# Latent attention with dispatch: another order of the steps on four engines

## The chip, the cores and the metric

The kernel runs on one core of one Trainium2 chip, as one program. The metric is the device time of a run in microseconds (us). TensorE (PE) does matrix products, VectorE (DVE) and ScalarE (ACT) do elementwise work and reductions and can read PSUM, GpSimd (POOL) works on SBUF and issues the indirect DMAs, SyncE (SP) issues plain DMAs. Each engine runs its own instructions strictly in their written order and waits on semaphores for the others.

## The reference

Activations x are 32 batches of 128 rows by 128 channels; a context is 32 x 128 x 96. Six residual stages follow each other, each on the layernorm of x. The fifth and the sixth are the ones the change concerns:

```
x = x + attn0(ln(x)); x = x + xattn0(ln(x), ctx); x = x + experts0(ln(x)); x = x + causal_attn(ln(x))
x = x + latent(ctx, ln(x), mask)      # 2 heads of 64; keys: 128 context rows + 128 rows of x itself
        q, k, v from layernorms; q and k RMS-normalised; softmax over 256 keys; times Wo
x = x + relu_moe(ln(x))               # router: 8 experts, top 2; relu(x w1 + b1) w2 + b2, gated sum
```

## The kernel before

The setup, four earlier stages and then the function `latent_attention` run one after the other. `latent_attention` works batch by batch (n from 0 to 31) and some steps by groups G of four batches. Beside the attention it does the dispatch for the last stage: it normalises the finished rows, computes router logits, ranks each row within its expert and scatters the rows to a DRAM buffer `routed`, where tiles of 256 rows of one expert are then read back by the last stage (`relu_experts`: 39 tiles, two products with four slices each, and two indirect DMAs per tile that write the results to `returned`).

The order on each engine is written out in a table, `ORDERS["latent"]`. An entry such as `K+2` in round n does step K of batch n+2, in each round. An entry such as `C^10` does the step of a group once, in the round where n+10 is the first batch of the group; for the steps `L`, `R`, `R1`, `EX`, `GG` and `PL` it is done for a unit of the router, in the round where n minus the number is the unit's last batch. The router's units are groups 0 and 1, 2 and 3, 4 and 5, 6, and 7. The loop goes over n from -14 to 55, on all engines with the same table, but each engine has its own n: nothing but semaphores ties the rounds together. A later round on POOL can therefore run at the same time as an earlier round on PE.

Per batch the steps on PE are P (L1707 to L1709, projections of x and of the context), K (L1767, three transposes of unit keys and queries), s (L1775 and L1777, scores and mask for the maximum), m (L1795, transpose of the maxima), T (L1707 to L1709 with q and k, the transposed scores), f (L1800, subtracts the maximum), w (L1811, probabilities by values), o (L1818, transpose of the heads), y (L1823 and L1824, output product). Per group: C and X (L1719, transposes of the normalised inputs), Z (L1726, transposes of the rows to be routed). Per unit: L (L1735, router logits, one product with a 128x8 output per batch, which the trace records as two) and R (L1743 and L1746, ranks by a triangular matrix). The semaphores that bind PE: T waits for `q_lo` and `k_lo`, K for `unit` of its batch and `k_lo` of the batch before, w for the exponentials.

The steps of the others that are spoken of: DVE R1 (L2090 to L2120, the router's choice of two, 14 instructions), sp (L2038, spreads the maximum), d (L2018, `q_heads`), M (L2026), n (L2047, L2049, heads), a (L2032), u (L2009, `unit`), ss (L1996 and L2001, `norms` and `norms_kept`), kl (L2056, `k_lo`), zm and zs (moments and shift of the finished rows), PL (places; for unit 2 also the list of the first 16 tiles), GG (gates, and labels into the rows). ACT kh (L1881 and L1882, rounded keys and queries), e (L1873 and L1874), zn (L1926, writes the normalised rows into a ring of four buffers), rp, zk (L1938). POOL rs (L2287 to L2295), iv (L2316, `inverse`), ql (L2309, `q_lo`), lc and lx (L2302, `c_lo` and `x_lo`), zr (L2326 and L2329), sc (L2339, two indirect DMAs of one batch).

The dispatch is bound by these waits: sc of batch n waits for PL and GG of its unit and for rp of its group. zn of group G waits, from group 4 on, until all scatters of group G-4 have landed, since it takes their buffer. SP starts the first 16 tiles when the scatters of groups 0 to 5 have landed (`EARLY_GROUPS = 6`). On POOL the sends of the last stage stand behind all 64 scatters.

Of the kernel before, what the change touches and what calls it, by code (L numbers as in the profile page):

```python
# [17 lines left out]
ACT, ALU, AX = mybir.ActivationFunctionType, mybir.AluOpType, mybir.AxisListType  # L18

P = 128  # L20
# [91 lines left out]
def load_setup(nc, x, weights, cols, rows, consts, later, sb, sem, ready, routed):  # L112

    with ExitStack() as ctx:
# [102 lines left out]
    },  # L217
    "latent": {
# [4 lines left out]
    },  # L223
}

# [2333 lines left out]
```

## Time and profile before

| | us |
|---|---|
| median of 3 runs | 1393.14 |
| lowest and highest | 1386.01, 1399.97 |
| profiled execution, its own time | 1390.87 |
| its span, first to last instruction | 1389.1 |
| attention and dispatch, first instruction to the last scatter of group 5 | 952 to 1203 |
| busy over the span: PE, DVE, ACT, POOL | 1192.9, 883.4, 677.0, 776.2 |

Of the span, 952 us belong to the stages in front, which the change does not touch, then some 250 us to attention and dispatch up to the first tile, and the rest to the tiles and the final sums. The share of busy time is therefore read stage by stage. A row of the timeline gives start and length in us, the engine, the source line, what is written and read, and in brackets how long the engine sat idle before and for whom. A row of the windows gives the busy time of each engine in one stretch and the clock granted to TensorE as a share of its full speed. Matmuls overlap, so the time of a step on PE is the distance between starts.

### The profile page before, as it was taken

The page shows a single profiled execution, that of the slowest core. Times are in us where ns is not written, and L with a number is a line of the kernel's source. Part 1 is how long each engine was busy: PE and PEld are TensorE (multiplying, and loading weights), DVE is VectorE, ACT ScalarE, POOL GpSimd, SP SyncE. Part 2 cuts the span into 40 slices and gives each one's busy share as a digit, 9 for nine tenths or more (in the row PEclk, how much of TensorE's full clock was granted, in tenths as well). Part 3 has the DMA queues.
Part 4 walks back from the last instruction along what each step waited for, and adds up shares of the span by engine and source line. Part 5 has one row for each costly group of instructions (what it writes and reads, how often), then busy time and mean ns, then how long its engine had stood idle before and what let it go on. Part 6 is the DMA issues. An engine that isn't in the chain of part 4 may idle for free. (4 is left out here: it accounts for less than half of the span.)

```text
span 1389.1 us, 34193 instructions
## 1 busy us (share of the span) xinstructions
PE 1192.9 (86%) x12731; PEld 902.3 (65%) x12731; DVE 883.4 (64%) x2024; ACT 677.0 (49%) x1304; POOL 776.2 (56%) x878
## 2 busy tenths in 40 slices
PE   1899998888888876999789999994799998399992
PEld 0577776656555555666457777773699997388882
DVE  3688876579999985677335665663688876422223
ACT  1344544434455433455334555544778653155561
POOL 3787775555555633444355655642676676765552
PEclk9999999689999997999958999997899897599996
DMA  9920000000000000000000000000000000366665
GB/s 345 381 79 2 3 2 8 9 15 15 21 16 15 10 9 1 1 1 1 1 1 2 3 2 3 2 3 15 17 13 7 11 23 32 124 202 202 196 196 187
DMA packets 51571, 75.46 MB, mean 54 GB/s; under 512 B 13118, under 2 KB 31683, under 8 KB 51152
## 3 DMA queue, kind: packets, MB, share of 16 engines
q1 hardware_dynamic: 43344, 60.57, 13.8%
q0 software_dynamic: 4544, 8.47, 1.8%
q10 hardware_dynamic: 3520, 4.23, 0.9%
q8 instruction: 104, 1.70, 0.5%
q14 instruction: 59, 0.48, 0.1%
HBM read 40.37 MB, written 31.70 MB: 52 GB/s over the span
## 5 line engine op out<-in xcount | busy, mean ns | idle before, releaser
L597 DVE TENSOR_REDUCE maxes<-bank 128x8 f32<-128x1024 f32 x192 | 234.4, 1221 | 58.7 <-PE bank L396 57.4
L524 ACT ACTIVATE self_probs<-bank 128x1024 f32<-128x1024 f32 x128 | 129.1, 1022 | 45.6 <-PE bank L428 45.2
L1468 POOL DMA_INDIRECT returned<-relu_y,relu_slots x78 | 76.3, 979 | 68.8 <-DVE relu_y L1444 54.8
L1405 ACT ACTIVATE relu_hidden<-bank,cols 128x256 f32<-128x256 f32 x156 | 73.8, 473 | 77.6 <-PE bank L1364 77.6
L738 POOL TENSOR_TENSOR self_k_hi_m<-self_kq_hi,const 128x512 fp32r<-128x512 f32 x64 | 66.5, 1039 | 80.0 <-ACT self_kq_hi L552 80.0
L531 ACT ACTIVATE self_neg_max<-bank 128x512 fp32r<-128x512 f32 x64 | 38.2, 596 | 148.0 <-PE bank L442 148.0
L1364 PE MATMUL bank<-latent_kq,relu_w_tile 128*128 128x256 f32 x312 | 94.8, 387 | 0.5 <-DVE latent_kq L1438 0.5
L1372 PE MATMUL bank<-relu_hidden,relu_w_tile 128*128 128x256 f32 x312 | 93.1, 381 | 0.0
L607 DVE RECIPROCAL self_recip<-bank 128x128 f32<-128x128 f32 x64 | 61.2, 956 | 31.6 <-PE bank L455 29.3
L1438 DVE COPY latent_kq<-bank 128x256 f32<-128x256 f32 x39 | 16.6, 425 | 100.5 <-PE bank L1354 98.1
L603 DVE TENSOR_SCALAR bank<-bank 128x1024 f32<-128x1024 f32 x64 | 78.2, 1223 | 3.3 <-PE bank L416 3.3
L738 POOL TENSOR_TENSOR causal_q_lo_m<-causal_kq_lo,const 128x512 fp32r<-128x512 f32 x32 | 33.3, 1040 | 80.5 <-PE bank L428 80.4
L2339 POOL DMA_INDIRECT routed<-latent_rows,latent_place_i x64 | 63.7, 995 | 24.4 <-issue 22.6
L455 PE MATMUL bank<-self_probs,values 128*32 128x128 f32 x2048 | 73.6, 287 | 1.4 <-ACT self_neg_max L531 1.2
L455 PE MATMUL bank<-self_probs,head_ones 128*32 128x128 f32 x2048 | 71.3, 282 | 0.0
L428 PE MATMUL bank<-self_neg_max,const_r 32*128 32x512 f32 x256 | 62.3, 478 | 9.2 <-DVE bank L603 5.7
L455 PEld LDWEIGHTS bank<-self_probs,values 128*32 128x32 f32 x2048 | 55.3, 114 | 18.9 <-issue 16.2
L524 ACT ACTIVATE causal_probs<-bank 128x1024 f32<-128x1024 f32 x64 | 64.5, 1021 | 6.0 <-PE bank L428 3.4
L738 POOL TENSOR_TENSOR self_q_lo_m<-self_kq_lo,const 128x512 fp32r<-128x512 f32 x64 | 66.5, 1039 | 0.4 <-PE bank L428 0.2
L738 POOL TENSOR_TENSOR self_q_hi_m<-self_kq_hi,const 128x512 fp32r<-128x512 f32 x64 | 66.4, 1038 | 0.0
L442 PE MATMUL bank<-ident,maxes 128*128 128x128 f32 x384 | 65.5, 295 | 0.6 <-POOL maxes L761 0.3
L1372 PEld LDWEIGHTS bank<-relu_hidden,relu_w_tile 128*128 128x128 f32 x312 | 59.7, 192 | 8.4 <-ACT relu_hidden L1405 0.2
(395 smaller groups left out, 3501.8 us busy)
## 6 DMA issues: line engine op xcount, KB each, us to landing
relu_w_tile<-in_w_ffn SPq DMA_DIRECT2D x39, 512.0 KB, 3.5
routed<-blank SPq DMA_DIRECT2D x1, 19760.0 KB, 61.2
relu_slots<-routed SPq DMA_DIRECT2D x39, 130.0 KB, 3.1
x_all<-in_x SPq DMA_DIRECT2D x8, 256.0 KB, 8.4
x_before<-x_all SPq DMA_DIRECT2D x8, 256.0 KB, 2.3
relu_back<-returned SPq DMA_DIRECT2D x4, 512.0 KB, 8.0
latent_mask_rows<-returned ACTq DMA_DIRECT2D x4, 512.0 KB, 8.7
self_ctx_in<-in_ctx SPq DMA_DIRECT2D x8, 192.0 KB, 2.5
```

Source lines behind the costliest of these rows:

```text
L428: mm = pe.matmul(t_bank(u), cr[rows_of(u), C_ONES + u * P:C_ONES + (u + 1) * P], neg_max[n % 2][rows_of(u), :], start=False, stop=True, sk ...
L442: mm = pe.transpose(OM[:, j * P:(j + 1) * P], maxes[n % 2][:, j * P:(j + 1) * P], sb["ident"][:, :])
L455: mm = pe.matmul(OM[rows_of(u), c:c + P], of(u, j), probs[n % 2][:, u, j, :], start=j == 0, stop=j == U - 1)
L524: act.activation(probs[n % 2][:, 2 * pair:2 * pair + 2, :, :].rearrange("p u j q -> p (u j q)"), T[:, 2 * pair * GT:(2 * pair + 2) * GT], ...
L597: dve.tensor_reduce(out.rearrange("p j u -> p u j"), S.rearrange("p (u j k) -> p u j k", u=2, j=U), AX.X, ALU.max, negate=True).then_inc(m ...
L603: dve.tensor_scalar(t, t, CLAMP / scale, -CLAMP / scale, ALU.min, ALU.max).then_inc(clipped, 1)
L738: pool.tensor_tensor(out[n % 2][:, :, :], src[(n // GB) % 2][:, batch_cols(n)].bitcast(F32).unsqueeze(1).broadcast_to([P, U, P]), slots.un ...
L1364: pe.matmul(HT[i % 2][:, 0:TT], w_tile[t % NW][:, c * P:(c + 1) * P], s[t % 2][:, :], start=True, stop=True)\
L1372: pe.matmul(YT[t % 2][:, 0:TT], w_tile[t % NW][:, F1 + c * P:F1 + (c + 1) * P], hidden[i % C1][:, :], start=c == 0, stop=c == C1 - 1).then ...
L1405: act.activation(hidden[i % C1][:, :], HT[i % 2][:, 0:TT], ACT.Relu, bias=sb["cols"][:, bass.ds(r + (COL_RELU + c), 1)]).then_inc(hidden_d ...
L1468: pool.indirect_dma_start(returned[:, :], bass.IndirectOffsetOnAxis(ap=slots[t % NX][:, b, P:P + 1].bitcast(I32), axis=0), y[t % NY][:, b, ...
L2339: pool.indirect_dma_start(routed[:, :], bass.IndirectOffsetOnAxis(ap=place_i[u % 3][:, k, b:b + 1], axis=0), rows[G % 4][:, k, n % GB, :], ...
```

## The change

Only the table `ORDERS["latent"]` changes. No instruction is added, removed or resized. On every engine the steps of a round stand in another order, and some are moved by one or more rounds. On POOL the scatter's number goes from 20 to 23.

```diff
     "latent": {
-        "PE": "T+0 m+0 K+2 w-1 y-2 f+0 L^-9 Z^-11 R^-10 P+5 C^10 o-1 s+2 X^9",
-        "ACT": "cp+4 ln^10 hc^8 ax^8 zn^-11 cn^11 sq+4 hx^8 kh+2 e+0 rp^-17 zk^-11 v+5 oc-1 EX^-10 ac^10",
-        "DVE": "mx^13 zs^-8 sp+0 d+2 M+1 n-1 a-2 u+3 ss+4 kl+2 zm^-5 PL^-10 R1^-9 GG^-11 mc^13",
-        "POOL": "lc^6 lx^5 ql+0 iv+2 rs^11 sc-20 zr^-7",
+        "PE": "K+2 m+0 w-1 T+0 C^9 y-2 L^-9 f+0 P+5 o-1 s+2 X^9 R^-10 Z^-10",
+        "ACT": "cp+4 zn^-9 hc^8 ax^8 kh+2 sq+4 ac^9 e+0 oc-1 hx^8 rp^-17 cn^11 EX^-10 ln^10 zk^-10 v+5",
+        "DVE": "R1^-10 sp+0 d+2 M+1 zs^-8 PL^-11 n-1 a-2 u+3 kl+2 ss+4 mc^13 GG^-11 mx^14 zm^-5",
+        "POOL": "lc^4 iv+0 rs^9 sc-23 ql-1 zr^-10 lx^4",
     },
```

The first place is PE around the ranks of unit 0 (R). In the kernel before, from the end of one T to the next P:

```order
L1709 MATMUL bank<-latent_q_hi,latent_k_lo 128x256
L1795 MATMUL bank<-ident,latent_maxes 32x128
L1767 MATMUL bank<-ident,latent_unit 128x128 x3
L1811 MATMUL bank<-latent_v,latent_probs 128x65 x4
L1823 MATMUL bank<-rows,latent_one 128x128
L1824 MATMUL bank<-raw_xattn,latent_o_t 128x128
L1800 MATMUL bank<-latent_neg_max,const_r 128x256 x2
L1743 MATMUL bank<-latent_both,const_r 128x64
L1746 MATMUL bank<-latent_both,const_r 128x56
```

In the changed kernel, from the end of s and the start of R:

```order
L1775 MATMUL bank<-latent_k_hi,latent_q_hi 128x256
L1777 MATMUL bank<-latent_mask_rows,const_r 128x128
L1743 MATMUL bank<-latent_both,const_r 128x64
L1746 MATMUL bank<-latent_both,const_r 128x56
```

R stood behind m, K, w, y and f; now it stands behind s, with K, m and w after it and then T. T itself has moved from the head of the round to between w and y, in every round, so that K, m and w stand between s and T, and only y, L and f between T and P.

The second place is POOL at group 2, behind the reciprocal deviations (rs) of group 3; the piece of the difference:

```order
 L2295 TENSOR_TENSOR latent_shift_ln<-latent_shift_ln,latent_rstd 128x8
+L2309 TENSOR_TENSOR latent_q_lo<-latent_q_heads,latent_q_hi 128x256
 L2302 TENSOR_TENSOR latent_c_lo<-latent_cf,latent_c_hi 96x512
-L2309 TENSOR_TENSOR latent_q_lo<-latent_q_heads,latent_q_hi 128x256
-L2316 TENSOR_TENSOR latent_inverse<-latent_norms_kept,latent_power 128x6
+L2316 TENSOR_TENSOR latent_inverse<-latent_norms_kept,latent_power 128x6
+L2309 TENSOR_TENSOR latent_q_lo<-latent_q_heads,latent_q_hi 128x256
 L2302 TENSOR_TENSOR latent_x_lo<-latent_xf,latent_x_hi 128x512
```

`q_lo` is now ahead of `c_lo` and of `x_lo`. The third place is POOL around the scatter of the batch that closes group 1 (the second row of each, two DMAs) and zr of group 5. Before:

```order
L2316 TENSOR_TENSOR latent_inverse<-latent_norms_kept,latent_power 128x6
L2339 DMA routed<-latent_rows,latent_place_i 38912x130 x2
L2326 TENSOR_SCALAR latent_z_var_eps<-latent_z_mean_var 128x4
L2329 TENSOR_TENSOR latent_z_rstd<-latent_z_var_eps,latent_power 128x4
L2309 TENSOR_TENSOR latent_q_lo<-latent_q_heads,latent_q_hi 128x256
```

Now:

```order
L2316 TENSOR_TENSOR latent_inverse<-latent_norms_kept,latent_power 128x6
L2339 DMA routed<-latent_rows,latent_place_i 38912x130 x2
L2309 TENSOR_TENSOR latent_q_lo<-latent_q_heads,latent_q_hi 128x256
L2326 TENSOR_SCALAR latent_z_var_eps<-latent_z_mean_var 128x4
L2329 TENSOR_TENSOR latent_z_rstd<-latent_z_var_eps,latent_power 128x4
```

zr has moved behind `q_lo`. The `inverse` in the first row is that of batch 29 before and of batch 30 now: since iv, ql and sc all changed their numbers, by 2, 1 and 3, the scatters and zr are one batch later against the work of the attention, not three.

## Rows read from the trace of the kernel before

**Rows 1.** Windows: engines' busy times, granted clock (PEclk), DMA share, GB/s.

```profile
core 0: us, PE busy (x) PEld busy (x) DVE busy (x) ACT busy (x) POOL busy (x), PEclk, DMA share, GB/s
1020.00:1040.00 20.00, 19.90 (x147) 18.02 (x146) 17.96 (x66) 16.24 (x51) 13.98 (x18) 1.00 0.02 5
...
1078.00:1080.00 2.00, 2.00 (x10) 2.00 (x10) 1.61 (x6) 0.00 (x0) 1.83 (x2) 0.50 0.03 8
...
1088.00:1090.00 2.00, 2.00 (x10) 2.00 (x9) 1.90 (x13) 0.42 (x4) 1.57 (x3) 0.50 0.00 0
...
1180.00:1200.00 20.00, 7.02 (x30) 6.31 (x30) 12.65 (x77) 3.59 (x9) 13.28 (x14) 0.50 0.45 149
```

**Rows 2.** Timeline of PE, two w steps in a row, plain rounds.

```profile
1032.86 1.00 PE L1811 MATMUL bank<-latent_v,latent_probs 128*128 128x65 f32 x8
...
1037.76 1.00 PE L1811 MATMUL bank<-latent_v,latent_probs 128*128 128x65 f32 x8
```

**Rows 3.** Timeline of PE, w steps with L and R between them.

```profile
1074.61 1.00 PE L1811 MATMUL bank<-latent_v,latent_probs 128*128 128x65 f32 x8
...
1084.34 1.12 PE L1811 MATMUL bank<-latent_v,latent_probs 128*128 128x65 f32 x8
...
1086.79 1.15 PE L1746 MATMUL bank<-latent_both,const_r 128*128 128x56 f32 x9
...
1092.03 1.00 PE L1811 MATMUL bank<-latent_v,latent_probs 128*128 128x65 f32 x8
...
1126.29 1.95 PE L1735 MATMUL bank<-cols,latent_x_t 128*128 128x8 f32 x16
1132.32 1.03 PE L1811 MATMUL bank<-latent_v,latent_probs 128*128 128x65 f32 x8
...
1139.91 1.00 PE L1811 MATMUL bank<-latent_v,latent_probs 128*128 128x65 f32 x8
```

**Rows 4.** Timeline at the start of the attention: POOL, DVE, PE.

```profile
993.68 1.26 POOL L2302 TENSOR_TENSOR latent_c_lo<-latent_cf,latent_c_hi 96x512 fp32r<-96x512 f32 x1
994.91 0.73 POOL L2309 TENSOR_TENSOR latent_q_lo<-latent_q_heads,latent_q_hi 128x256 fp32r<-128x256 f32 x1
995.61 1.32 POOL L2316 TENSOR_TENSOR latent_inverse<-latent_norms_kept,latent_power 128x6 f32<-128x6 f32 x1
...
995.75 0.42 DVE L2018 TENSOR_TENSOR latent_q_heads<-bank,latent_head_gamma 128x256 f32<-128x256 f32 x1 [1.84 <-POOL latent_q_lo L2309]
...
997.09 1.50 DVE L2009 TENSOR_TENSOR latent_unit<-latent_kq,latent_inverse 128x384 f32<-128x384 f32 x1
...
997.23 0.33 PE L1818 MATMUL bank<-ident,latent_heads 128*128 128x128 f32 x1 [1.10 <-DVE latent_heads L2049]
...
999.72 0.52 PE L1767 MATMUL bank<-ident,latent_unit 128*128 128x128 f32 x3 [0.88 <-DVE latent_k_lo L2056]
```

**Rows 5.** Timeline where scatters, `x_lo` and the norms meet: DVE, POOL, PE.

```profile
1111.18 1.72 DVE L2001 TENSOR_SCALAR latent_norms_kept<-latent_norms 128x6 f32<-128x6 f32 x1
...
1111.53 1.29 POOL L2302 TENSOR_TENSOR latent_x_lo<-latent_xf,latent_x_hi 128x512 fp32r<-128x512 f32 x1
...
1113.37 0.52 PE L1767 MATMUL bank<-ident,latent_unit 128*128 128x128 f32 x3 [0.59 <-DVE latent_k_lo L2056]
```

**Rows 6.** Timeline of the end of the attention: PE, then POOL.

```profile
1164.08 0.66 PE L1726 MATMUL bank<-ident,latent_rows 128*128 128x128 f32 x4
...
1208.12 0.66 PE L1354 MATMUL bank<-ident,relu_slots 128*128 128x128 f32 x2 [12.65 <-DMA relu_slots<-routed]
...
1175.90 0.19 POOL L2326 TENSOR_SCALAR latent_z_var_eps<-latent_z_mean_var 128x4 f32<-128x4 f32 x1 [5.36 <-DVE latent_z_mean_var L2070]
...
1182.75 1.06 POOL L2339 DMA_INDIRECT routed<-latent_rows,latent_place_i  x1 [5.54 <-issue]
...
1201.95 0.96 POOL L2339 DMA_INDIRECT routed<-latent_rows,latent_place_i  x1 [0.30 <-issue]
```

**Rows 7.** DMA issues: count, median us from issue to landing.

```profile
routed<-latent_rows,latent_place_i POOLq DMA_INDIRECT x64, 2.4
```

## The prediction, as it was put on record before the result

> **What bounds the kernel now.** I read the windows first, to see which stage has idle engines. In plain rounds of the attention TensorE is busy 19.90 of 20 us at full clock, VectorE 17.96, POOL 13.98 [rows 1]. A round there takes 4.90 us, the distance of two w steps [rows 2]. The order of work cannot shorten that: no matmul is removed, and TensorE waits for nothing. What is left to win or lose is where TensorE idles or runs slowly, and there are four such places.
>
> The first is the start, where the chain of waits goes over POOL, VectorE and TensorE: q_lo at 994.91 stands behind c_lo, VectorE sits idle 1.84 us for it, and TensorE is idle 1.10 us before o and 0.88 us before K [rows 4]. The second is the granted clock. It falls to 0.50, the lower level of 1.2 GHz, in the rounds that hold L and R, although TensorE is busy 2.00 of 2.00 us there [rows 1]. The third is one round in the stretch of the scatters, where TensorE is idle 0.59 us before K [rows 5]. The fourth is the end, from the last attention step to the first tile at 1208.12, where TensorE had been idle 12.65 us for the first rows read back [rows 6], at half clock and busy 7.02 of 20 us [rows 1].
>
> **The change, part by part.** The sum is made against the profiled execution, 1390.87 us with a span of 1389.1, which is 2.3 us under the median of 1393.14.
>
> *Ranks and the clock.* In the order before, the steps m, K, w, y, f and then L or R follow each other between the dense products T and P. All these are small outputs, one-row weights or transposes. The w steps around R are 1084.34 and 1092.03, 7.69 us apart, and again 1132.32 and 1139.91, 7.59 apart [rows 3]. A plain round is 4.90 [rows 2] and R takes 1.15 of it [rows 3], so 6.05 would be the price at full clock and 1.64 and 1.54 us are lost to the half clock, 3.2 in all. Now R stands behind s, and K, m and w follow, then T. The run of small work around R shrinks from m, K, w, y, f, R to R, K, m, w. Two of its six parts are gone and dense work stands on both sides. I take it that these two falls go: **minus 3.2 us**. The bounds are 0, if they stay, and a gain of 3.2.
>
> *Logits and the clock.* L stood behind m, K, w, y, f, now behind y alone, in front of f. The w steps around the first L are 1074.61 and 1084.34 [rows 3], 9.73 us apart; 4.90 for the round [rows 2] and 1.95 for an L at full clock [rows 3] make 6.85, so 2.9 us are lost to the fall. L itself is the longest stretch of tiny outputs in the kernel and its neighbours on both sides are still y and f. I take 0, since the L step is untouched in length, and keep a gain of 5.8 (two units) as a bound.
>
> *The start.* q_lo of batch 2 passes ahead of c_lo and comes 994.91 - 993.68 = 1.23 us earlier; q_heads, the maximum and the heads behind it on VectorE follow. But T and m used to run before K, and now K is the first step of the round. K waits for the unit keys, whose inverse still stands behind c_lo: 995.61 + 1.32 = 996.93, then 1.50 for the product [rows 4] and about 0.4 for k_lo, now directly behind it, about 998.8. Before, K began at 999.72. TensorE is 0.9 us earlier at K, but still has T to do, some 0.7 us. I take **minus 0.5**, with 0 and 2.0 (the two idle times) as bounds. On VectorE k_lo now stands in front of the two norms, which costs the inverse of a later batch 0.4 us; the inverse is wanted a round later.
>
> *The collision at 1111.* norms_kept takes 1.72 us while x_lo runs on POOL for 1.29, and k_lo and K queue behind it [rows 5]. Now k_lo is in front of the norms, so such a collision no longer reaches K, and x_lo is behind q_lo. **Minus 0.6**, bounds 0 and 0.8.
>
> *K at the head of each round.* K is asked for about 0.8 us (T and m) earlier in its round, and k_lo comes earlier by the norms that it passed. Where the unit product meets a POOL instruction it takes up to 1.50 us [rows 4] instead of some 0.55, and then K may wait a few tenths. **Plus 0.5**, bounds 0 and 3 (a tenth in each of 30 rounds).
>
> *The scatters.* Against the attention's own steps they move by one batch, not by three. When the attention ends POOL thus has one more batch to send, two DMAs of 1.28 us each by the 15 distances between the 16 issues from 1182.75 to 1201.95 [rows 6]: 2.6 us. POOL sits idle 5.36 and then 5.54 us before the scatter of batch 16 at 1182.75 [rows 6], because places and gates of unit 2 are late, not POOL. 2.6 of 10.9 us are hidden. The 16 scatters from there to 1201.95 decide when the tiles start and are the same as before, and so is the order of L, R, R1, PL and GG among themselves behind the last batch. Cost 0. If the cover were gone, it would be 2.6. zr is one batch later too; its user, the shift on VectorE, now meets it nearly at once, but stands behind d, which waits for the same q_lo. Cost 0.
>
> *The last rounds.* There a round waits for the exponentials. The rows' transpose Z of group 5, at 1164.08 [rows 6], stood between the last f and w and now falls into the wait of the round before. It takes some 0.5 us, so **minus 0.5**, bounds 0 and 0.5.
>
> *ScalarE.* Normalisations move behind the keys and the exponentials. TensorE did not wait for them in plain rounds, so 0.
>
> The sum is -3.2 - 0.5 - 0.6 + 0.5 - 0.5 = **-4.3 us**: 1386.6 in the profiled execution, 1388.8 against the median. I forecast **1389**.
>
> One rule speaks against the largest term. TensorE showed no idle time in the windows where its clock fell [rows 1]. The Trainium skill, page "TensorE: Matmul & The Clock Gate", section "HAM oscillation — how this bites in real kernels", lays such falls to gaps in which the array waits idle. By that rule moving work that is already gapless wins nothing, and the sum would be 1.1 us instead of 4.3. The trace disagrees with it in so far as the falls came without a gap; what it would take to avoid them no row shows.
>
> **The rivals.**
>
> *The falls stay.* The clock could go by what L and R are, not by what stands before them. For it: both rounds with R and both with L show a fall, and none of the plain ones. Against it: R is a shorter step than L, and its fall is separate from that of L, with full clock in between. The time is then 1393.1 - 1.1 = 1392.
>
> *More falls go.* If the breaking up of the small work is what counts, the two L rounds are helped as well: 5.8 us more, and the logits of unit 2 perhaps 1.5. 1389 - 7.3 = 1381.5. Against it: y, L and f still stand together.
>
> *New falls (slower).* In plain rounds P, o, s and T were one dense run, and T is now cut off from it and stands alone between w and y. No plain round of the kernel before has T there, so nothing shows that the clock holds. A fall costs about 1.6 us by the rounds with R. The gain of 4.3 is used up by three falls. With one in every second round, 14 of them, it is 14 x 1.6 = 22 us less 1: about 1414; with one per group of four, 7 x 1.6 - 1 = +10, 1403. Against it: the same work is done in the same 4.90 us, and its longest run of small steps gets shorter. I take 1403 as this rival's time.
>
> *ScalarE held by the ring (slower, small).* zn of groups 4 and 5 stood in a round where its buffer's scatters had long landed; it is now two rounds earlier, in front of kh and e, and the scatters are a batch later. The landing takes 2.4 us [rows 7], and by my count some 2 us are left at each. Were POOL 5 us later than I reckon, 3 us would be lost twice, and the sum would be +2: 1395.
>
> **How the numbers follow.** Chances: my forecast 0.44 (1389), the falls stay 0.28 (1392), more falls go 0.13 (1381.5), new falls 0.08 (1403), ScalarE held 0.07 (1395). A median of three runs moves too: the runs before reach from 1386 to 1400. Eight in ten are in 1379 to 1399, which takes in the bounds of the sum (all gains without L: -6.5; none and K's full cost: +3), the case of more falls and that of the ring, and leaves out most of the new falls. About one per cent, 14 us, is what can be told from no change. Faster than 1379.2 needs the third case and a lucky median: 0.08. Slower than 1407 needs the new falls in more than every fourth round: 0.05. The rest, 0.87, is the same within 1%.
>
> **What would show it.** In the profile of the changed kernel the first step holds if the window after R shows clock 1.00 and the w steps around R are about 6.1 us apart; it fails if 0.50 stands there. The rounds with L should still show 9 to 10 us. K should show no idle time for k_lo in the stretch of the scatters. The scatter of batch 16 should still follow idle time on POOL, and begin some 4 us earlier than 1182.75; if POOL is busy up to it, the scatters have become the bound. Clock 0.50 in plain rounds is the fourth case, and ScalarE idle before zn for a DMA the fifth. The prediction is wrong as a whole if the plain round is not 4.90 us, since everything rests on the order leaving that alone.

## The result

The changed kernel takes 1411.43 us (median of 3 runs, 1404.64 to 1417.99), against 1393.14 before: ratio 1.0152, 95% interval 1.0095 to 1.0208. A second measurement gave 1.0103 (1.0044 to 1.0163); the execution profiled there took 1426.97 us, over 1.5% above the fastest of its kernel, and is not in that ratio. The change is slower by 1.0 to 1.5%, where I forecast no change.

The profiled execution of the changed kernel is its slowest run, 1417.99 us with a span of 1416.2, which is 27.1 us over the span before. Before, the attention's first w step stood at 993.6 and its last at 1165.0, 171.4 us; now 997.96 and 1192.40, 194.4 us. That is 23.0 of the 27.1. The attention starts 5.4 us later, in stages that the change does not touch, and the remaining pieces add up to -1.3. So the question is what happened between the first w and the last.

### The profile page after: what moved, and what is told of

It reads as the page before. It is cut to its first block and busy times, and to the rows that moved or that the text cites. A ratio compares the mean times of both kernels' runs of the same rounds, so it can differ in the third digit from the quotient of the medians.

```text
span 1416.2 us, 34193 instructions
## 1 busy us (share of the span) xinstructions
PE 1221.5 (86%) x12731; PEld 925.2 (65%) x12731; DVE 883.7 (62%) x2024; ACT 677.2 (48%) x1304; POOL 777.4 (55%) x878
## 5 line engine op out<-in xcount | busy, mean ns | idle before, releaser
L738 POOL TENSOR_TENSOR self_q_lo_m<-self_kq_lo,const 128x512 fp32r<-128x512 f32 x64 | 66.6, 1040 | 3.0 <-PE bank L428 2.8
L442 PEld LDWEIGHTS bank<-ident,maxes 128*128 128x128 f32 x384 | 43.9, 148 | 33.9 <-issue 28.0
```

The lines of the kernel that those rows point to most:

```text
L442: mm = pe.transpose(OM[:, j * P:(j + 1) * P], maxes[n % 2][:, j * P:(j + 1) * P], sb["ident"][:, :])
L738: pool.tensor_tensor(out[n % 2][:, :, :], src[(n // GB) % 2][:, batch_cols(n)].bitcast(F32).unsqueeze(1).broadcast_to([P, U, P]), slots.un ...
```

## The profile after

The page of the changed kernel. Second line: the granted clock in 40 slices of 35.4 us.

```profile
PE 1221.5 (86%) x12731; PEld 925.2 (65%) x12731; DVE 883.7 (62%) x2024; ACT 677.2 (48%) x1304; POOL 777.4 (55%) x878
PEclk9999999689999996999859999996799777599996
```

TensorE is busy 28.6 us longer than before with the same 12731 instructions; VectorE, ScalarE and POOL are within 1.2 us of before. TensorE did not wait more, it worked more slowly. The windows of the attention say where (columns as in [rows 1]):

```profile
1000.00:1020.00 20.00, 18.05 (x79) 15.63 (x78) 11.45 (x35) 11.03 (x34) 8.68 (x8) 0.62 0.04 11
...
1040.00:1060.00 20.00, 19.80 (x143) 17.59 (x143) 18.18 (x62) 17.19 (x56) 14.16 (x17) 1.00 0.05 11
...
1100.00:1120.00 20.00, 20.00 (x90) 18.33 (x90) 10.58 (x42) 10.70 (x33) 5.37 (x6) 0.57 0.00 1
...
1160.00:1180.00 20.00, 19.84 (x103) 17.44 (x104) 12.23 (x42) 7.63 (x24) 10.04 (x12) 0.70 0.04 14
```

Between 1040 and 1060 all is as before. Between 1100 and 1120 TensorE is busy 20.00 of 20 us and does 90 matmuls instead of some 145. Closer, in windows of 3 us:

```profile
1090.00:1093.00 3.00, 3.00 (x25) 2.84 (x24) 2.77 (x6) 0.69 (x2) 2.85 (x4) 1.00 0.04 8
1093.00:1096.00 3.00, 3.00 (x19) 2.94 (x18) 2.59 (x13) 2.56 (x10) 1.32 (x1) 0.57 0.00 0
...
1105.00:1108.00 3.00, 3.00 (x16) 2.94 (x16) 1.90 (x6) 1.50 (x5) 0.39 (x1) 0.50 0.00 0
...
1114.00:1117.00 3.00, 3.00 (x17) 2.94 (x15) 1.19 (x3) 2.81 (x10) 0.00 (x0) 0.50 0.00 0
1117.00:1120.00 3.00, 3.00 (x19) 2.44 (x19) 1.11 (x5) 1.54 (x4) 1.94 (x3) 0.95 0.03 8
```

The clock falls to 0.50 (1.2 GHz) about 1093.4 and comes back at 1117.3: 24 us without a moment of idle time. In the kernel before it fell at L and once more at R, and each time it was back in 3 to 7 us. The timeline of TensorE over this stretch, w steps with what stands between them, after two w steps of plain rounds:

```profile
1045.06 1.00 PE L1811 MATMUL bank<-latent_v,latent_probs 128*128 128x65 f32 x8
1049.97 1.04 PE L1811 MATMUL bank<-latent_v,latent_probs 128*128 128x65 f32 x8
...
1087.55 1.00 PE L1811 MATMUL bank<-latent_v,latent_probs 128*128 128x65 f32 x8
...
1089.99 1.85 PE L1735 MATMUL bank<-cols,latent_x_t 128*128 128x8 f32 x16
...
1094.80 1.81 PE L1811 MATMUL bank<-latent_v,latent_probs 128*128 128x65 f32 x8
...
1102.99 2.06 PE L1746 MATMUL bank<-latent_both,const_r 128*128 128x56 f32 x9
...
1105.82 1.81 PE L1811 MATMUL bank<-latent_v,latent_probs 128*128 128x65 f32 x8
...
1113.84 1.07 PE L1726 MATMUL bank<-ident,latent_rows 128*128 128x128 f32 x4
...
1115.56 1.81 PE L1811 MATMUL bank<-latent_v,latent_probs 128*128 128x65 f32 x8
```

The plain round is 4.91 us, against 4.90 [rows 2]. The distances from 1087.55 on are 7.25 (with L), 11.02 (with R) and 9.74 us (with Z), against 9.73, 7.69 and 5.33 before. The R of 1102.99 takes 2.06 us instead of 1.15 [rows 3]: it is inside the slow stretch. The same comes again at the L of 1144.77, with the distances 7.40, 11.02 and 9.74. The 23.0 us, worked out from the distances of the w steps of both kernels:

| rounds | before | after | more |
|---|---|---|---|
| 2 to 5 of the attention | 23.6 | 31.3 | 7.7 |
| the four from the first L on | 28.4 | 34.7 | 6.2 |
| the four from the second L on | 25.1 | 33.2 | 8.1 |
| the last four | 15.8 | 16.9 | 1.1 |
| the other 15 | 78.5 | 78.4 | -0.1 |

The first line is the start. There K waits for k_lo, and behind it the clock falls for 20 us (the window 1000 to 1020 above). POOL, VectorE and TensorE:

```profile
999.71 1.28 POOL L2302 TENSOR_TENSOR latent_c_lo<-latent_cf,latent_c_hi 96x512 fp32r<-96x512 f32 x1
1000.95 1.32 POOL L2316 TENSOR_TENSOR latent_inverse<-latent_norms_kept,latent_power 128x6 f32<-128x6 f32 x1
...
1002.30 1.14 DVE L2009 TENSOR_TENSOR latent_unit<-latent_kq,latent_inverse 128x384 f32<-128x384 f32 x1 [1.02 <-POOL latent_inverse L2316]
...
1003.92 0.52 PE L1767 MATMUL bank<-ident,latent_unit 128*128 128x128 f32 x3 [1.85 <-DVE latent_k_lo L2056]
```

The idle time itself, 1.85 us, is as long as the 1.10 and 0.88 of before together [rows 4]. Between 1006 and 1190 TensorE waits for almost nothing; the view of waits gives in total, times and longest:

```profile
PE bank L1795 <- ACT latent_o_t L1951: 0.6, 2, 0.3
PE bank L1823 <- DVE latent_neg_max L2038: 0.4, 2, 0.2
```

K's wait of [rows 5] is gone. The end of the attention, TensorE and then POOL:

```profile
1192.40 1.97 PE L1811 MATMUL bank<-latent_v,latent_probs 128*128 128x65 f32 x8 [0.49 <-ACT latent_probs L1874]
...
1236.10 0.66 PE L1354 MATMUL bank<-ident,relu_slots 128*128 128x128 f32 x2 [12.02 <-DMA relu_slots<-routed]
...
1204.51 0.20 POOL L2326 TENSOR_SCALAR latent_z_var_eps<-latent_z_mean_var 128x4 f32<-128x4 f32 x1 [4.38 <-DVE latent_z_mean_var L2070]
...
1211.37 1.06 POOL L2339 DMA_INDIRECT routed<-latent_rows,latent_place_i  x1 [5.54 <-issue]
```

From the last w to the first tile it is 43.7 us, and was 43.1. POOL is idle 4.38 and 5.54 us before the scatter of batch 16, as in [rows 6]: it was not held up by the one batch more that it had to send.

## The experiments

Eighteen runs, in five groups, the kernels of a group on one chip with the kernel before. On the chip of the second group all kernels ran some 24 us longer, the kernel before 1417.43, so only ratios to it are compared. "Mean clock" below is the granted clock over 30 us from L on; (1 - clock) x 2 x 30 is the time at 0.50.

The yardstick, the kernel before and the changed one at the first and the second L:

```profile
1077.00:1107.00 30.00, 30.00 (x191) 28.14 (x191) 23.73 (x78) 20.46 (x65) 18.18 (x18) 0.83 0.03 11
1126.00:1156.00 30.00, 29.79 (x196) 27.09 (x196) 23.58 (x86) 14.70 (x48) 22.36 (x24) 0.89 0.08 26
```

```profile
1090.00:1120.00 30.00, 30.00 (x144) 27.30 (x143) 18.43 (x67) 15.65 (x48) 11.49 (x13) 0.60 0.01 2
1145.00:1175.00 30.00, 29.95 (x141) 27.14 (x140) 18.84 (x70) 12.21 (x40) 17.31 (x18) 0.60 0.06 19
```

Before 0.83 and 0.89: 10 and 7 us at 0.50, in two pieces each. Changed 0.60 and 0.60: 24 us each.

### T alone, each way

Between T and P of the changed kernel C stands too, once in four rounds, beside y, L and f, and X, R and Z stand between s and K in some rounds. All of them stay there in e1, the changed kernel with T back at the head.

```diff
-        "PE": "K+2 m+0 w-1 T+0 C^9 y-2 L^-9 f+0 P+5 o-1 s+2 X^9 R^-10 Z^-10",
+        "PE": "T+0 K+2 m+0 w-1 C^9 y-2 L^-9 f+0 P+5 o-1 s+2 X^9 R^-10 Z^-10",
```

> The changed kernel with T alone put back to the head of TensorE's round (T K m w C y L f P o s X R Z); ScalarE, VectorE and POOL as changed. Theory A (T cut off from P, o, s leaves the clock at 0.50 for 20 to 24 us after each L instead of 3 to 7): P, o, s and T are neighbours again but for R and Z once in a while, the clock comes back within about 7 us of each L, the attention from the first to the last w takes about 171 to 175 us instead of 194, and the time is 1390 (1386 to 1395). Rival B (the loss comes from the order of the other engines or from the scatters 23 behind): the low stretches stay 20 us or longer and the time stays near 1411. Rival C (L alone decides, by chance of its moment): anything between, with one low stretch of about 20 us more or less, 9 us each.

Measured: 1393.82 us against 1395.52, ratio 0.9985 (0.9955 to 1.0014). First to last w 168.7 us. The windows behind its two L:

```profile
1086.00:1116.00 30.00, 29.43 (x208) 27.03 (x208) 25.02 (x84) 22.58 (x71) 18.85 (x19) 0.94 0.02 6
1132.00:1162.00 30.00, 29.10 (x189) 26.30 (x189) 22.70 (x82) 15.59 (x50) 21.72 (x22) 0.89 0.07 24
```

0.94 and 0.89 are 4 and 7 us at half clock. One step put back takes the whole loss away, with the scatters still 23 behind and three engines as changed. Rival B falls.

```diff
-        "PE": "T+0 m+0 K+2 w-1 y-2 f+0 L^-9 Z^-11 R^-10 P+5 C^10 o-1 s+2 X^9",
+        "PE": "m+0 K+2 w-1 T+0 y-2 f+0 L^-9 Z^-11 R^-10 P+5 C^10 o-1 s+2 X^9",
```

> The kernel before with T alone moved from the head of TensorE's round to between w and y (m K w T y f L Z R P C o s X). Theory A: the whole loss appears with this one step, low stretches of about 20 us at each L (and, here, at R), the attention takes 190 to 200 us from first to last w, time 1410 (1403 to 1418). Rival B: T is harmless, the time stays at 1393 (1388 to 1398). Rival C: between, since m still stands directly behind s and K is not at the head.

Measured: ratio 1.0146 (1.0094 to 1.0198), first to last w 194.3 us. Its window at L and its largest wait between 990 and 1200:

```profile
1087.00:1117.00 30.00, 29.68 (x177) 27.01 (x176) 21.39 (x75) 19.18 (x59) 16.25 (x17) 0.77 0.03 8
```

```profile
PE bank L1795 <- ACT latent_o_t L1951: 5.8, 17, 0.7
```

The size came as theory A says, but only a part in its way. The clock is 0.77 and 0.72 behind the two L, 14 and 17 us, and the plain round is 5.38 to 5.58 us instead of 4.90: m now stands directly behind s and waits for ScalarE to copy o out of their common bank, 5.8 us in all, and K waits for k_lo, 2.6 us. In the changed kernel K stands between s and m and covers the first of these waits. Of the 22.9 us that e2 takes longer from first to last w than the kernel before, 8.1 lie in the eight rounds from the two L on (14.3 in the changed kernel), 3.7 at the start, 5.3 in the 15 other rounds, where the waits are, and 5.8 in the last four.

### TensorE's row against the other three

e3 is the changed kernel with TensorE's row of before (C^9 and Z^-10 kept), e4 the kernel before with TensorE's row of the change (C^10, and Z^-11 in front of P).

> The changed kernel with the whole order of TensorE as before (T m K w y f L Z R P C o s X; C and Z at the numbers that the changed ScalarE needs); ScalarE, VectorE, POOL and the scatters as changed. Theory A: TensorE's row carries the whole loss, so the time is that of the kernel before or 1 us less (the start and the collision of my prediction): 1389 to 1394, with both falls at R back. Rival B (the other engines or the scatters): about 1405 to 1411, with TensorE idle for something, or POOL busy right up to the scatter of batch 16.

> The kernel before with TensorE's order as changed (K m w T C y L f Z P o s X R; C and Z at the numbers that ScalarE needs); ScalarE, VectorE, POOL and the scatters 20 behind as before. Theory A: about 1411 (1404 to 1418), three stretches of 20 to 24 us at clock 0.50 in the attention. Rival B: 1393 (1388 to 1398). Together with the run before it this splits the change by engine; the two differences from the kernel before should add up to that of the change.

Measured: e3 1.0051 (1.0016 to 1.0086), e4 1.0129 (1.0057 to 1.0201). TensorE's row carries most of it. The other engines alone are no gain but a small loss: in e3 X, in the same round as C and behind s, waits five times for ScalarE's copies, 2.2 us in all, and every fourth round is 6.6 us, where the round with C and X is 5.7 in e1. In e4 K waits nine times for k_lo, 7.1 us in all, and the first L leaves 20 us at half clock, the second only 3:

```profile
1092.00:1122.00 30.00, 30.00 (x154) 27.35 (x155) 20.12 (x71) 16.30 (x53) 13.75 (x14) 0.66 0.02 5
1148.00:1178.00 30.00, 28.83 (x197) 25.58 (x197) 23.75 (x86) 14.56 (x47) 22.74 (x24) 0.94 0.08 27
```

So a T cut off makes the long stretch likely, not certain. The two losses, 0.5% and 1.3%, add up to 1.8%, against 1.5% and 1.0% for the whole change.

### R, the scatters, and how far T may stand from s

e5 is the kernel before with R^-10 moved to the end of TensorE's row, f5 the kernel before with sc-23.

> The kernel before with R alone moved from in front of P to behind s (and X); T stays at the head of the round, so R stands between s and T. My prediction's first step: both falls at R go, the two w distances at R become about 6.1 us instead of 7.6, time 3.2 us less: 1392 by a kernel before of 1395. Rival: R makes its fall wherever it stands, distances of 7.6 stay, 1395. Falls at L stay in both.

Measured: 0.9987 (0.9957 to 1.0016). R's own falls are gone, its w distances are 6.74 and 6.57 us, but L's fall now lasts 7 us both times, with distances of 9.12 and 9.29 us against 9.73 and 8.22 before. The three distances from each L on add up to 21.2 and 20.8 us, against 22.8 and 20.7 before: 1.5 us of the expected 3.2, all at one of the two.

> The kernel before with the scatter's number alone changed from 20 to 23, so that each batch's two DMAs are issued three rounds later against POOL's other steps. My step 'The scatters' says that one batch later is hidden under POOL's idle time of 10.9 us before the scatter of batch 16; three batches are 7.7 us of sending at the end of the attention, still within it: no change, ratio 0.998 to 1.002. If the scatters bound the first tile it is 3 to 8 us slower: ratio 1.002 to 1.006. Clock stretches as before.

Measured: 1.0011 (0.9975 to 1.0047). The scatter's number changes nothing that these runs can show. At the second L of this run the clock did not fall at all (w distances 6.68 and 6.54), with the same row on TensorE.

f1 puts T behind m (`K+2 m+0 T+0 w-1`), so that only K and m separate it from s:

> The changed kernel with T moved up past w only (K m T w C y L f P o s X R Z): K and m, some 0.5 us at full clock, stand between s and T. Theory A (the clock comes back only after a long enough run of dense products): the split is short, so I expect low stretches in between, 7 to 15 us at each L, and 1393 to 1403. If a single small step between s and T is enough to keep the clock down, 1411. If it is harmless, 1393 as with T at the head.

```profile
1083.00:1113.00 30.00, 29.71 (x211) 27.34 (x211) 26.15 (x85) 22.19 (x70) 18.61 (x19) 0.94 0.02 6
1129.00:1159.00 30.00, 28.74 (x197) 25.77 (x197) 25.52 (x90) 16.93 (x54) 23.76 (x24) 0.94 0.08 26
```

Measured: 0.9984 (0.9949 to 1.0019), 4 us at each L, first to last w 172.8 us. K and m do no harm between s and T. The changed kernel differs from f1 by nothing but w in front of T.

### L elsewhere

f2 has T at the head and L behind P, f3 T as changed and L behind P (`T+0 C^9 y-2 f+0 P+5 L^-9 o-1`).

> The changed kernel with T at the head of the round and L moved from in front of f to between P and o (T K m w C y f P L o s X R Z). Theory A with L as the trigger: L now has dense products on both sides instead of y and f; either no fall at L (the round with L 6.9 us instead of 9 or so, 2 to 3 us less at each of two L, 1389 to 1391 by a kernel before of 1395), or the fall comes anyway and, since L now cuts the dense run in which the clock came back, the stretch is as long as before or longer: 1394 to 1398.

> The changed kernel with L alone moved to between P and o; T stays between w and C (K m w T C y f P L o s X R Z). It separates trigger from recovery. If L between y and f is the trigger, no long stretch starts in the middle of the attention and the time drops to about 1393 (first to last w about 172 us) although T is still cut off. If L makes the clock fall wherever it stands, the two stretches of 20 us or more stay and it is 1411. If the order with T cut off loses the clock even without L, there are stretches in plain rounds.

Measured: f2 1.0034 (1.0000 to 1.0069), a fall of 3 us at each L and another two rounds on. f3 1.0105 (1.0053 to 1.0157), w distances 7.23, 11.02 and 9.74 at its first L, with no wait of TensorE between 1080 and 1120:

```profile
1087.00:1117.00 30.00, 30.00 (x148) 27.46 (x147) 19.04 (x67) 15.80 (x49) 10.20 (x12) 0.60 0.00 1
1142.00:1172.00 30.00, 29.92 (x147) 27.26 (x146) 19.09 (x70) 11.60 (x38) 16.74 (x18) 0.60 0.06 19
```

L makes the clock fall between dense products too. Where T is cut off it stays down.

### L in pieces

Does it need L in one piece? Its eight products were split, with the rows `... f+0 P+5 L^-9 o-1 s+2 L2^-9 X^9 R^-10 Z^-10`, T where the change has it (g2) or at the head (g1), and in quarters (g3):

```diff
-                for i, G in enumerate(UNITS[u]):
-                    for b in range(GB):
...
+                mine = [(i, G, b) for i, G in enumerate(UNITS[u]) for b in range(GB)]
+                mine = mine[len(mine) * part // parts:len(mine) * (part + 1) // parts]
+                for i, G, b in mine:
```

> The changed kernel with the eight products of L given in two halves, four between P and o and four between s and K (K m w T C y f P L o s L2 X R Z); T still between w and C, not one product more or less. Theory A (the trigger is the 1.85 us of tiny outputs in one piece; the state then persists because T is cut off): with halves of 0.9 us the clock does not fall, the stretches of 24 us are gone, first to last w about 167 to 172 us, ratio to the kernel before 0.998 to 1.002. Rival: L makes the clock fall in halves too, and the stretches stay: 1.010 to 1.015.

> The changed kernel with T at the head of the round and L in two halves, between P and o and between s and T. If halves avoid the fall: no low stretch at L, rounds with L 6.9 us, first to last w 163 to 166 us, ratio 0.994 to 0.997, the fastest so far. If they fall all the same: the round with L and the next together about 15 us as with L in one piece, ratio 0.998 to 1.003.

> The same with L in four quarters, behind P, o, s and behind the next T. As the halves if these avoid the fall already (0.994 to 0.997); if the halves fall and the quarters do not, the length of the piece of tiny outputs sets it; if both fall, L's products cost the clock however they are spread (0.998 to 1.003).

Measured: g2 1.0097 (1.0071 to 1.0124), g1 1.0052 (1.0024 to 1.0081), g3 1.0107 (1.0050 to 1.0163). In all three the round with L is 6.6 us long at full clock: in pieces L does not make the clock fall. But the clock falls in the next round, where a wait is new. Windows of g1, then VectorE's first step of R1 and the next sp, then TensorE's y (in these kernels the source lines lie 3 to 5 further down):

```profile
1086.00:1090.00 4.00, 4.00 (x33) 3.87 (x34) 3.11 (x8) 2.50 (x10) 3.81 (x5) 1.00 0.00 2
1090.00:1094.00 4.00, 2.06 (x18) 1.94 (x17) 3.59 (x16) 1.61 (x6) 0.37 (x1) 0.92 0.00 0
1094.00:1098.00 4.00, 4.00 (x14) 3.33 (x14) 3.59 (x8) 1.77 (x5) 1.96 (x2) 0.50 0.02 4
```

```profile
1089.71 0.23 DVE L2095 TENSOR_TENSOR latent_logits<-bank,rows 128x64 f32<-128x64 f32 x1 [0.74 <-PE bank L1737]
...
1093.15 0.41 DVE L2043 TENSOR_TENSOR latent_neg_max<-bank,const 32x256 fp32r<-32x256 f32 x1
...
1093.70 0.76 PE L1826 MATMUL bank<-rows,latent_one 1*128 1x128 f32 x2 [1.94 <-DVE latent_neg_max L2043]
```

The last products of L come later, R1 at the head of VectorE's round waits for them and takes 3.4 us, the maximum (sp) stands behind it, and y idles 1.94 us for it. There the clock falls, and it stays down for 17 us with T at the head too. In this stretch R stands between s and T. Four kernels tried to take that wait away: R1 behind M (h1, and h2 with T as changed), the halves of L one place earlier (h3), R1 behind ss (h4).

> T at the head, L in halves behind P and behind s as in g1, and on VectorE R1 moved behind sp, d and M, so that y's bank and f no longer wait for R1's 14 instructions. If the idle 1.94 us was the trigger in g1: no stretch at clock 0.50 at either L, first to last w 163 to 167 us, ratio 0.993 to 0.997. If the halves of L or R themselves bring the clock down: low stretches of 3 to 17 us remain, ratio 0.999 to 1.006.

> The changed kernel, T still between w and y, with L in halves and R1 behind M. If L in one piece (or the wait that replaced it) is the only trigger: no stretch in the middle, first to last w 165 to 172 us, ratio 0.994 to 1.001. If the order with T cut off falls by itself or R does it: ratio 1.005 to 1.015.

> T at the head, the halves of L in front of f and behind P (not behind s), R1 at the head of VectorE's round as changed. The logits are done some 1.5 us earlier than in g1, so the wait of y shrinks from 1.94 to about 0.5 us. If that wait was the trigger, no fall or a short one, ratio 0.994 to 0.999; if the first half beside y and f is enough for a fall, the round with L is 8 to 9 us and the ratio 0.998 to 1.002.

> As h1 with R1 behind ss, the last of the batch's steps on VectorE. TensorE's R, at the end of its round, then waits for R1's last result, by my count 1 to 2 us, and an idle wait there should bring the clock down once per unit: ratio 0.997 to 1.004, slower than h1. If R's wait does not matter for the clock, as h1.

Measured: h1 1.0149 (1.0068 to 1.0230), h2 1.0172 (1.0083 to 1.0262), h3 1.0100 (1.0005 to 1.0195), h4 1.0139 (1.0055 to 1.0224). None gave the gain that I had hoped for. How large the losses are is uncertain: the kernel before ran at some 1380 us in three of its seven runs of this group, and its median was 1392.45, while in the 14 runs of the next group, on the same chip, it took 1385.75 to 1402.87, median 1395.13. R1's 14 instructions only handed the wait on: in h1 o waits 3.7 us for x_all, which is now behind R1, in h4 R waits for R1, up to 3.5 us, and the clock falls 10 to 17 us each time. h3 had its falls of 3 us at L and at Z (8.05, 6.08 and 7.70 us), as its second expectation had it, and the same 168.7 us from first to last w as e1; its ratio, from four runs, is too wide to set it apart. So "the trigger removed" was not reached, and whether a cut-off T costs nothing without a fall is shown only by the plain rounds, 4.91 us.

### T at the other end

i1 puts T directly in front of f and P, so that it touches the dense run from the other side; i2 is the changed kernel again, on the same chip.

> The changed kernel with T alone moved further back, to between L and f (K m w C y L T f P o s X R Z), so that T, f, P, o and s are one run with K, m and w behind it. Theory A (the clock comes back in the first unbroken run of dense products): the stretches at clock 0.50 after L are 3 to 7 us, first to last w 168 to 173 us, ratio to the kernel before 0.997 to 1.002. Rival (T has to follow s ahead of K, as in all fast orders so far): stretches of 20 us or more, ratio 1.010 to 1.016.

> The changed kernel unaltered, on the same chip as i1 and the kernel before. By its first measurement: ratio 1.010 to 1.021, two stretches of 24 us at clock 0.50, w distances of 11.0 and 9.7 us behind each L. A ratio below 1.005 would mean that the first measurement was chance.

```profile
1083.00:1113.00 30.00, 30.00 (x147) 27.54 (x147) 19.66 (x71) 15.66 (x49) 10.77 (x11) 0.60 0.00 1
1138.00:1168.00 30.00, 30.00 (x145) 27.46 (x145) 19.25 (x70) 11.62 (x40) 16.95 (x18) 0.60 0.06 19
```

Measured: i1 1.0082 (1.0042 to 1.0123), 0.60 and 0.60 again; i2 1.0103 (1.0044 to 1.0163), w distances 11.02 and 9.74 behind both L. My theory in its simple form missed: with f alone between T and P the stretches stay. (A wait of y is also new here, twice 0.83 us, with a fall of 3 us behind the second; TensorE waits for nothing in the two long stretches.)

## Why the prediction was wrong

**What is shown.** L (or an idle wait near it) brings the clock down in nearly all orders. How long it stays down depends on where T stands. Going through the clock of all profiled kernels from 1030 us on, as long as P is in the round: where T follows s with nothing or only K, m or Z between, it came back within 3 to 7 us, in 24 of 24 falls. Where R stood between s and T in that stretch, all eight falls (g1, g3, h1, h4) lasted 10 to 17 us. With w between, or f between T and P, fourteen of seventeen lasted 14 to 24 us. Outside that part the rule does not hold. At the start the fall lasted 10 us in e5 and f1, with T behind s or behind K and m, and 3 us in f3, with T cut off; in the last rounds, where P is gone, the clock of h1 was down from 12 us before the last w on, with T at the head.

That T, by its place, sets the size of the loss is shown by e1 and f1 one way, and, with a wait beside it, by e2 the other. The 14.3 us at the two L are 1.0% of the time; the 7.7 us of the start, which vary, are most of the rest. Why K and m may stand there and w or f may not is open; so is why single falls fail to come (f5) or end early (e4, g2). Whether R and Z behind s, as in the changed kernel, lengthen a stretch was not run by itself: it lasted 14 and 17 us in e2, where R stands in front of P, and 24 in the changed kernel. They are not enough for it, since e1 has them too.

Step by step:

- **Ranks and the clock** (-3.2): the mechanism holds in part. R makes no fall of its own behind s, but e5 measured 1.5 us less, not 3.2, because the fall at the second L lasted longer instead. In the changed kernel R lies in the long stretch, so nothing of the gain came.
- **Logits and the clock** (0): this is the step that failed. I wrote "I take 0, since the L step is untouched in length". The falls at L did stay, and I let them keep their 2.9 us each, with a gain as the only bound. (The second L cost less than I took: its w distance was 8.22, 1.4 us over the 6.85, so the bound for two was 4.3, not 5.8.) But those 2.9 us were the price of a fall plus its recovery, and the recovery leaned on T, directly behind s, which the change takes away. The rounds from the two L on took 6.2 and 8.1 us more. The move of T itself had no term in the sum.
- **The start** (-0.5): K waits 1.85 us where o and K had waited 1.98, so the idle time is 0.1 us less, not 0.5. The fall behind it lasted 20 us instead of 3, and these rounds took 7.7 us more. That T's place did this is not shown: the length varies from run to run, 10 us in the second trace of the changed kernel and 10 in e5 and f1 too.
- **The collision at 1111** (-0.6) and **K at the head** (+0.5): no wait of K after 1006, a plain round 0.01 us longer, and the 15 other rounds, in which both lie, 0.1 us shorter, as the two terms add up.
- **The scatters** (0): right, by POOL's idle time after and by f5.
- **The last rounds** (-0.5): wrong in sign, +1.1; the cause was not looked for.
- **ScalarE** (0): right; TensorE waits for it 0.6 us in all (the view of waits above).

The rival "New falls" named the cause, T cut off from P, o and s, and came nearest in time (1403), but with 8 in 100, and priced as falls in plain rounds, of which there are none. I had asked whether the clock would fall, and never when it would come back. The trace was there: in the kernel before each low stretch at L or R ends within the next T or shortly behind it, at the first w. The text said that the prediction is wrong as a whole if the plain round is not 4.90; it is 4.91, and the forecast was wrong all the same, since the long stretches lie in the rounds with L, R and Z.

On the page's rule that I weighed: the Trainium skill, "TensorE: Matmul & The Clock Gate", section "HAM oscillation — how this bites in real kernels", lays the loss of the clock to gaps in which the array waits. g1 agrees, its fall stands in 1.94 us of idle time; the changed kernel does not, its clock fell and stayed at 0.50 with TensorE busy 3.00 of 3.00 us.

No order tried beats the kernel before: e1, f1 and e5 lie within 0.2% of it, with intervals on both sides of 1.

## What to carry to other kernels

Where the granted clock falls under a busy TensorE, read two things: which step it falls behind, and which step it comes back behind. A reordering that leaves the first alone can still remove the second; here a fall of 3 to 7 us became one of 24. Try first to keep the densest products of a round next to each other behind the step at which the clock falls, and measure it: here T close behind s was enough, T close in front of P was not. And before spreading a long step over the round look at who waits for its last piece.

## What was unexpected in the hardware

- The clock stayed at 0.50 for 24 us of gapless work, three rounds in a row, twice in each of the two traces of the changed kernel, while the plain round of the same order runs at full clock in 4.91 us. In plain rounds of that order the clock fell only at the start, behind K's wait, and there it stayed down through a plain round of 8.6 us as well.
- The same L, with the same row on TensorE, cost a fall or none (f5), and in eight products spread over the round it cost none in any of the six traces with all its pieces behind P (rounds of 6.6 to 6.7 us).
